# Layer norms from a statistics instruction per 128-column block and one finishing pass shared by two engines

## The chip, the cores and the metric

The kernel runs on one core of one Trainium2 chip. The metric is the time of one execution on the device in microseconds (us), the median of several executions. A profile is one further execution with the hardware profiler on.

## What is computed

The reference runs four graph layers on 6250 nodes of 128 features and 206250 edges, with a layer norm after each of them:

```python
def _layernorm(x, axis=-1, eps=1e-05):
    m = jnp.mean(x, axis=axis, keepdims=True)
    v = jnp.var(x, axis=axis, keepdims=True)
    return (x - m) / jnp.sqrt(v + eps)
...
x = _layernorm(x + _L0_gnn_ref(x, ..., edge_type_3, node_type_3), axis=-1)
x = _layernorm(x + _L1_gnn_ref(x, L1_gnn_weight, L1_gnn_bias, edge_index, edge_weight), axis=-1)
x = _layernorm(x + _L2_gnn_ref(edge_index, x), axis=-1)
x = _layernorm(x + _L3_gnn_ref(x, edge_attr_64, src, dst, 6250, ...), axis=-1)
```

The first layer is a message-passing layer by edge type and node type, the second a hyperbolic one (it begins with the logarithm map of the normed rows, so it needs their norm), the third a normalised sum over neighbours, the fourth a sum over neighbours and edge features with a matrix product and a ReLU.

## The kernel before

The 6250 nodes lie in SBUF as 49 blocks of 128 rows (NB = 49, D = 128): node b*128+p is in partition p, columns b*128 to b*128+127 of the tile `X`, which is 128 partitions by 6272 fp32 columns. `X3` and the other names that end in 3 are the same data seen as 128 x 49 x 128. `big` is one large scratch tile out of which each stage cuts what it needs; in the trace all those cuts are called big. `small` holds vectors of 128 x 49, one number for each node, and `sm(i)` is its i-th slot.

The program is a row of blocks (`nc.Block()`), each with one instruction stream for each engine, and all engines meet at a block's end. Most of the time goes to stages that build and multiply adjacency matrices on TensorE and gather rows on GpSimd. The norms stand between these stages. Norm 1 follows layer 0 and opens the block at L1641; norm 2 is in the block at L1863, behind the hyperbolic layer's last steps; norm 3 is in the block at L2085, a block of VectorE and ScalarE alone; norm 4 is in the last block (L2144), behind the final matrix products, and the store of the output follows it.

`layer_norm` (L665) is a chain on VectorE. It takes the sum of each block (L671; norm 4 has it already, from the accumulator of L2173), divides it (L672), subtracts the mean from all 6272 columns in place (L673), and calls `sum_of_squares` (L658): ScalarE squares the first SHARE = 18 blocks and sums each with its accumulator (L724), while VectorE multiplies the other 31 blocks by themselves (L661) and sums them (L662). Then come the variance (L675), the square root on ScalarE (L721), the reciprocal (L677), in norm 1 the function `logs` (L1650), and the scaling of all 6272 columns into X (L679). `link` makes VectorE wait for each instruction before it starts the next; `Chain` holds the jobs that VectorE asks of ScalarE (`ask`, `did`) and `answer` is ScalarE's side of it. `sum_of_squares` is also called twice outside the norms (L1712, L1871).

Of the kernel before, what the change touches and what calls it, by code (L numbers as in the profile page):

```python
# [20 lines left out]
ALU = mybir.AluOpType  # L21
ACT = mybir.ActivationFunctionType
AX = mybir.AxisListType

P = 128
N, E, D, T, FE = 6250, 206250, 128, 3, 64
NB = -(-N // P)
# [35 lines left out]
EPS = 1e-5  # L63
# [51 lines left out]
def at_least(eng, sem, value):  # L115

    if not isinstance(value, int) or value > 0:
        eng.wait_ge(sem, value)
# [8 lines left out]

BB = 4
SHARE = 18


def in_batches(eng, body):
# [13 lines left out]
def build(nc, x, src, dst, attr, etype, weight, ntype, w_e, b_e, w_n, b_n, w1, b1, w3, w3e, b3, out):  # L146
    ctx = ExitStack()
    with ctx:
        ctx.enter_context(nc.allow_non_contiguous_dma(reason="node types, leftover edges"))

        def sb(name, cols, dt=F32, rows=P):
            return ctx.enter_context(nc.sbuf_tensor(name, [rows, cols], dt))
# [24 lines left out]
        X3 = X[:, :].rearrange("p (b f) -> p b f", b=NB)  # L177
# [26 lines left out]
        small = sb("small", 20 * NB)  # L204
        degs = sb("degs", 6 * NB)
        indeg, outdeg, first_edge, next_edge, row_f, node_id = (degs[:, i * NB:(i + 1) * NB] for i in range(6))
        spill_row = sb("spill_row", NB, I32)
        owner = sb("owner", JB, I32)
        ramp = sb("ramp", P * TU, BF16)
# [439 lines left out]
        def sm(i):  # L649
            return small[:, i * NB:(i + 1) * NB]  # L650

        def along(v):
            return v.unsqueeze(2).to_broadcast([P, NB, D])

        def wide(v):
            return v.rearrange("p (b f) -> p b f", b=NB)

        def sum_of_squares(dve, link, h3, sq3, to):  # L658

            asked = chain.squares(h3, sq3, to)  # L660
            link(dve.tensor_tensor(sq3[:, SHARE:, :], h3[:, SHARE:, :], h3[:, SHARE:, :], ALU.mult))  # L661
            link(dve.tensor_reduce(out=to[:, SHARE:], in_=sq3[:, SHARE:, :], axis=AX.X, op=ALU.add))  # L662
            dve.wait_ge(chain.did, asked)

        def layer_norm(dve, link, h3, sq3, ask_sqrt, before_x=lambda: None, summed=False):  # L665

            mean, var = sm(0), sm(1)
            if not summed:  # L670
                link(dve.tensor_reduce(out=mean, in_=h3, axis=AX.X, op=ALU.add))  # L671
            link(dve.tensor_scalar(mean, mean, 1.0 / D, None, ALU.mult))  # L672
            link(dve.tensor_tensor(h3, h3, along(mean), ALU.subtract))  # L673
            sum_of_squares(dve, link, h3, sq3, var)
            link(dve.tensor_scalar(sm(2), var, 1.0 / D, EPS, ALU.mult, ALU.add))  # L675
            ask_sqrt(sm(2), sm(2))
            link(dve.reciprocal(sm(2), sm(2)))  # L677
            before_x()
            link(dve.tensor_tensor(X3, h3, along(sm(2)), ALU.mult))  # L679

        class Chain:

# [12 lines left out]
            def link(self, ins):  # L695
                self.n += 1
                ins.then_inc(self.v, 1)
                self.dve.wait_ge(self.v, self.n)
# [10 lines left out]
            def squares(self, h3, sq3, to):  # L709
# [3 lines left out]
                self.dve.sem_inc(self.ask, 1)  # L713
                return self.k

            def answer(self, act, first=0, last=None):

                for k, f, i, o, to in self.jobs[first:last]:
                    act.wait_ge(self.ask, k)
                    if f is not None:  # L720
                        act.activation(o, i, f).then_inc(self.did, 1)  # L721
                    else:
                        for b in range(SHARE):
                            made = act.activation(o[:, b, :], i[:, b, :], ACT.Square, accum_out=to[:, b:b + 1])  # L724
                        made.then_inc(self.did, 1)
# [13 lines left out]
        chain = Chain()  # L739
# [901 lines left out]
        with nc.Block() as block:  # L1641
            @block.vector
            def _(dve):
# [6 lines left out]
                def logs():  # L1650
# [8 lines left out]
                    chain.func(ACT.Ln, lo, lo)  # L1659
                    chain.func(ACT.Ln, hi, hi)  # L1660
                layer_norm(dve, link, h43, sq43, chain.sqrt, logs)
                dve.sem_inc(s_x1, 1)
                before_products.append(len(chain.jobs))
# [199 lines left out]
        with nc.Block() as block:  # L1863
            @block.vector
            def _(dve):
                chain.on(dve)
                link = chain.link
                raw, norm, th, f, ne = (sm(i) for i in range(3, 8))
                g = wide(agg7)

                sum_of_squares(dve, link, g, sq83, raw)  # L1871
                chain.sqrt(raw, raw)
                link(dve.tensor_scalar(norm, raw, MIN_NORM, None, ALU.max))
                chain.func(ACT.Tanh, norm, th)
# [260 lines left out]
        h123, sq123 = wide(h12), wide(sq12)  # L2135
# [8 lines left out]
        with nc.Block() as block:  # L2144
            @block.tensor
            def _(pe):
                pe.wait_ge(s_e_rows, 16)
                for b in range(NB):
                    to = ps[b % 8][:, 0:D]
                    at_least(pe, s_a12, b - 7)  # L2150
                    pe.matmul(to, flat[:, b * P:(b + 1) * P], w3s[:, :], start=True, stop=False)  # L2151
                    pe.matmul(to, e_rows[0:FE, b * P:(b + 1) * P], w3ew[:, :], start=False, stop=True).then_inc(s_o12, 1)  # L2152

            @block.vector
            def _(dve):
                chain.on(dve)
                link = chain.link
                for n in range(NB + 2):
                    if n < NB:
                        here = slice(n * D, (n + 1) * D)  # L2160
                        dve.wait_ge(s_o12, n + 1)
                        dve.tensor_tensor(h12[:, here], ps[n % 8][:, 0:D], gained[:, here], ALU.add).then_inc(s_a12, 1)  # L2162
                    if 1 <= n <= NB:
                        b = n - 1
                        here = slice(b * D, (b + 1) * D)
                        dve.wait_ge(s_a12, b + 1)
                        dve.scalar_tensor_tensor(h12[:, here], h12[:, here], degn[:, b:b + 1], b3b[:, :],  # L2167
                                                 ALU.mult, ALU.add).then_inc(s_h12, 1)
                    if n >= 2:
                        b = n - 2  # L2170
                        here = slice(b * D, (b + 1) * D)
                        dve.wait_ge(s_h12, b + 1)
                        dve.scalar_tensor_tensor(h12[:, here], h12[:, here], 0.0, X[:, here], ALU.max, ALU.add,  # L2173
                                                 accum_out=sm(0)[:, b:b + 1]).then_inc(s_r12, 1)
                dve.wait_ge(s_r12, NB)
                layer_norm(dve, link, h123, sq123, chain.sqrt, summed=True)
                dve.sem_inc(s_x4, 1)

            @block.scalar
            def _(act):  # L2180
                chain.answer(act)

            @block.sync
            def _(sp):
                sp.dma_start(e_rows[0:FE, :], e_sums).then_inc(s_e_rows, 16)
                sp.wait_ge(s_x4, 1)
                sp.dma_start(out[0:NFULL * P, :].rearrange("(b p) f -> p b f", p=P), X3[:, 0:NFULL, :]).then_inc(s_out, 16)
                sp.dma_start(out[NFULL * P:N, :], X3[0:NREST, NFULL, :]).then_inc(s_out, 16)
                sp.wait_ge(s_out, 32)
# [20 lines left out]
```

## Time and profile before

| | before |
|---|---|
| timed executions | 5433.2, 5448.58, 5449.89 us; median 5448.58 us |
| profiled execution, its own time | 5436.3 us |
| profiled execution, span | 5434.5 us |
| busy in the span | PE 4035.9 us (74%), DVE 3337.4 us (61%), POOL 2259.1 us (42%), ACT 1187.5 us (22%) |
| granted TensorE clock, mean | 0.932 |

PE is TensorE, DVE VectorE, ACT ScalarE, POOL GpSimd, SP the engine that issues most DMAs. A busy share is a mean over stages with different limits, so what a change in one stage is worth is read from the stretch in which it stands.

### The profile page before, as it was taken

The page shows a single profiled execution, that of the slowest core. Times are in us where ns is not written, and L with a number is a line of the kernel's source. Part 1 is how long each engine was busy: PE and PEld are TensorE (multiplying, and loading weights), DVE is VectorE, ACT ScalarE, POOL GpSimd, SP SyncE. Part 2 cuts the span into 40 slices and gives each one's busy share as a digit, 9 for nine tenths or more (in the row PEclk, how much of TensorE's full clock was granted, in tenths as well). Part 3 has the DMA queues.
Part 4 walks back from the last instruction along what each step waited for, and adds up shares of the span by engine and source line. Part 5 has one row for each costly group of instructions (what it writes and reads, how often), then busy time and mean ns, then how long its engine had stood idle before and what let it go on. Part 6 is the DMA issues. An engine that isn't in the chain of part 4 may idle for free. (4 is left out here: it accounts for less than half of the span.)

```text
span 5434.5 us, 110895 instructions
## 1 busy us (share of the span) xinstructions
PE 4035.9 (74%) x42529; PEld 2913.6 (54%) x42529; DVE 3337.4 (61%) x4224; ACT 1187.5 (22%) x2165; POOL 2259.1 (42%) x2066
## 2 busy tenths in 40 slices
PE   4367755555555554399999995499996799959996
PEld 3255555555555554388888874255554344424444
DVE  7796899898989988566666445666666300150004
ACT  0025555555555554300000000200001100010000
POOL 0051477777777777377777774000000021000200
PEclk9998899999999998799999998699998899979995
DMA  9547687777777778766666665388884566546661
GB/s 306 205 127 252 234 308 274 281 274 291 278 284 276 276 289 243 213 173 174 173 174 173 175 174 107 127 310 305 305 305 146 182 218 211 160 135 206 225 193 49
DMA packets 568380, 1196.81 MB, mean 220 GB/s; under 512 B 173529, under 2 KB 379949, under 8 KB 559117
## 3 DMA queue, kind: packets, MB, share of 16 engines
q1 hardware_dynamic: 481500, 1025.12, 54.4%
q0 software_dynamic: 71088, 153.71, 10.9%
q10 hardware_dynamic: 15660, 16.22, 1.0%
q8 instruction: 85, 1.39, 0.1%
q14 instruction: 47, 0.38, 0.0%
HBM read 767.29 MB, written 480.27 MB: 230 GB/s over the span
## 5 line engine op out<-in xcount | busy, mean ns | idle before, releaser
L1382 PE MATMUL psum<-big 128*128 128x98 bf16 x7936 | 871.9, 209 | 731.5 <-DVE big L1364 534.5
L1336 POOL DMA_INDIRECT big<-typed_msgs,big x1080 | 1258.7, 1165 | 372.6 <-issue 326.7
L1382 PEld LDWEIGHTS psum<-big 128*128 128x128 bf16 x7936 | 772.1, 98 | 782.5 <-issue 303.7
L1979 PE MATMUL psum<-big 128*128 128x512 bf16 (+1 forms) x4704 | 990.5, 374 | 140.4 <-DMA big<-adj 140.4
L1518 POOL DMA_INDIRECT big<-typed_msgs,big x760 | 775.6, 1021 | 322.2 <-issue 224.3
L1383 PE MATMUL psum<-big 128*128 128x49 bf16 x7936 | 858.9, 192 | 0.0
L1384 PE MATMUL psum<-big 128*128 128x49 bf16 x7936 | 855.9, 187 | 0.0
L1979 PEld LDWEIGHTS psum<-big 128*128 128x128 bf16 x4704 | 461.0, 98 | 665.1 <-DMA big<-adj 140.9
L1384 PEld LDWEIGHTS psum<-big 128*128 128x128 bf16 x7936 | 802.9, 102 | 0.0
L1383 PEld LDWEIGHTS psum<-big 128*128 128x128 bf16 x7936 | 776.6, 98 | 0.0
L2026 POOL DMA_INDIRECT big<-spill,spill_row x98 | 92.5, 943 | 1472.0 <-DMA spill<-big 1442.7
L1816 PE MATMUL psum<-big 128*128 128x416 f32 x1984 | 655.7, 494 | 63.5 <-DVE big L1850 62.5
L1364 DVE TENSOR_TENSOR big<-big 128x2400 bf16<-128x2400 bf16 x496 | 694.3, 1400 | 0.0
L1534 DVE SCALAR_TENSOR_TENSOR big<-iota,node,big 128x512 f32<-128x512 f32 x456 | 343.4, 753 | 424.8 <-PE psum L1615 366.5
L1361 DVE TENSOR_TENSOR big<-big 128x2048 bf16<-128x2048 bf16 x496 | 603.5, 1217 | 0.0
L1850 DVE STREAM_TRANSPOSE big<-big 128x3136 f32<-128x3136 f32 x124 | 427.2, 3445 | 239.3 <-PE psum L1816 220.5
L1411 ACT CAST big<-psum 128x784 bf16<-128x784 f32 x496 | 404.8, 816 | 767.4 <-PE psum L1384 486.0
L1615 PE MATMUL psum<-big 128*128 128x128 f32 x3648 | 531.9, 289 | 39.4 <-DMA big<-typed_msgs,big 39.4
L1816 PEld LDWEIGHTS psum<-big 128*128 128x128 f32 x1984 | 377.9, 191 | 340.9 <-issue 82.2
L1615 PEld LDWEIGHTS psum<-big 128*128 128x128 f32 x3648 | 444.6, 192 | 120.2 <-issue 71.4
L1611 PE MATMUL psum<-big 128*64 128x128 f32 x3648 | 498.8, 280 | 6.7 <-DVE big L1534 6.7
L1611 PEld LDWEIGHTS psum<-big 128*64 128x64 f32 x3648 | 388.6, 137 | 86.7 <-issue 43.0
(315 smaller groups left out, 3548.1 us busy)
## 6 DMA issues: line engine op xcount, KB each, us to landing
wadj<-big SPq DMA_DIRECT2D x248, 784.0 KB
big<-wadj SPq DMA_DIRECT2D x124, 1568.0 KB, 7.0
big<-adj SPq DMA_DIRECT2D x210, 896.0 KB, 4.7
adj<-big SPq DMA_DIRECT2D x62, 1568.0 KB
big<-staged SPq DMA_DIRECT2D x266, 256.0 KB
big<-edge_feats SPq DMA_DIRECT2D x456, 128.0 KB
edge_feats<-in_edge_attr SPq DMA_DIRECT2D x1, 51562.5 KB, 162.6
staged<-big SPq DMA_DIRECT2D x30, 1280.0 KB
```

The costliest lines, as they stand in the source:

```text
L1336: pool.indirect_dma_start(out=sgot4[:, c, u, :], out_offset=None, in_=typed_rows, in_offset=bass.IndirectOffsetOnAxis(ap=spair4i[:, c, u, ...
L1361: dve.tensor_tensor(lo_b[:, q, :, :].rearrange("p t (c d) -> p t c d", d=2), in_twos(lo_ramp).to_broadcast([P, TT, P // 2, 2]), all_column ...
L1364: dve.tensor_tensor(hi_b[:, q, :, 1:4, :].rearrange("p t s (c d) -> p t s c d", d=2), hi.unsqueeze(2).to_broadcast([P, TT, 3, HC // 2, 2]) ...
L1382: pe.matmul(to[:, 0:2 * NB], lo, hi_b[:, q, t, 0:2, 0:NB], start=True, stop=False)
L1383: pe.matmul(to[:, NB:2 * NB], lo, hi_b[:, q, t, 2, 0:NB], start=False, stop=False)
L1384: last = pe.matmul(to[:, NB:2 * NB], lo, hi_b[:, q, t, 3, 0:NB], start=False, stop=True)
L1518: pool.indirect_dma_start(out=got4[:, h, u, :], out_offset=None, in_=typed_rows, in_offset=bass.IndirectOffsetOnAxis(ap=pair4i[:, h, u, 0: ...
L1611: pe.matmul(ps[h][0:FE, D:ACCW], feat4[:, h, u, :], hot4[:, k, u, :], start=(u == 0), stop=(u == U - 1))
L1615: last = pe.matmul(ps[h][:, 0:D], hot4[:, k, u, :], got4[:, h, u, :], start=(u == 0), stop=(u == U - 1))
L1816: last = pe.matmul(ps[c][:, 0:(b1 - b0) * 32], rows, turned[:, n % RT, q * QROW + b0 * 32:q * QROW + b1 * 32], start=(m == 0), stop=(m == ...
L1850: dve.transpose(turned[:, n % RT, :].rearrange("p (h i) -> p h i", i=32), wring[:, n % RW, :].rearrange("p (h g) -> p h g", g=32)).then_in ...
L1979: last = pe.matmul(ps[c % 2][:, 0:len(blocks) * P], terms_[:, k, b * D:(b + 1) * D], ring_a[:, m % RA, 0:len(blocks), s * P:(s + 1) * P], ...
```

## The change

`layer_norm` no longer centres the rows nor squares them. VectorE runs its statistics instruction (`bn_stats`) once on each of the 49 blocks. Each gives six numbers for each row: count, mean and sum of squared deviations of the even columns, and the same of the odd columns. Five instructions on 128 x 49 vectors join the two halves into a mean and a sum of squared deviations, two more make the mean's final value and the variance. The square root and the reciprocal stay. One further instruction makes `shift`, minus the mean times the scale. The finishing pass is now one instruction for each block: ScalarE takes the first NORM_SHARE = 19 blocks as Identity with a scale and a bias for each partition (the new job `rows`), VectorE takes the other 30 as subtract and multiply with two scalars for each partition, and then waits for ScalarE. The tile `stats` is new. Norm 4 makes its sums again with the statistics, and L2173 still makes the sum that it no longer uses. `sum_of_squares` and its two other uses stay as they were.

```diff
+NORM_SHARE = 19
...
-            mean, var = sm(0), sm(1)
-            if not summed:
-                link(dve.tensor_reduce(out=mean, in_=h3, axis=AX.X, op=ALU.add))
-            link(dve.tensor_scalar(mean, mean, 1.0 / D, None, ALU.mult))
-            link(dve.tensor_tensor(h3, h3, along(mean), ALU.subtract))
-            sum_of_squares(dve, link, h3, sq3, var)
-            link(dve.tensor_scalar(sm(2), var, 1.0 / D, EPS, ALU.mult, ALU.add))
-            ask_sqrt(sm(2), sm(2))
-            link(dve.reciprocal(sm(2), sm(2)))
+            mean, raw, scale = sm(0), sm(1), sm(2)
+            for b in range(NB):
+                made = dve.bn_stats(stats3[:, b, :], h3[:, b, :])
+            link(made)
+            mean_e, sq_e, mean_o, sq_o = (stats3[:, :, j] for j in (1, 2, 4, 5))
+            link(dve.tensor_tensor(mean, mean_e, mean_o, ALU.add))
+            link(dve.tensor_tensor(scale, mean_e, mean_o, ALU.subtract))
+            link(dve.tensor_tensor(scale, scale, scale, ALU.mult))
+            link(dve.tensor_tensor(raw, sq_e, sq_o, ALU.add))
+            link(dve.scalar_tensor_tensor(raw, scale, D / 4.0, raw, ALU.mult, ALU.add))
+            link(dve.tensor_scalar(mean, mean, 0.5, None, ALU.mult))
+            link(dve.tensor_scalar(scale, raw, 1.0 / D, EPS, ALU.mult, ALU.add))
+            ask_sqrt(scale, scale)
+            link(dve.reciprocal(scale, scale))
+            link(dve.scalar_tensor_tensor(shift, mean, -1.0, scale, ALU.mult, ALU.mult))
             before_x()
-            link(dve.tensor_tensor(X3, h3, along(sm(2)), ALU.mult))
+            asked = chain.rows(h3, X3, scale, shift)
+            for b in range(NORM_SHARE, NB):
+                made = dve.tensor_scalar(X3[:, b, :], h3[:, b, :], mean[:, b:b + 1], scale[:, b:b + 1], ALU.subtract, ALU.mult)
+            link(made)
+            dve.wait_ge(chain.did, asked)
...
+                    if isinstance(f, tuple):
+                        for b in range(NORM_SHARE):
+                            made = act.activation(o[:, b, :], i[:, b, :], ACT.Identity, bias=f[1][:, b:b + 1], scale=f[0][:, b:b + 1])
+                        made.then_inc(self.did, 1)
```

The first place is VectorE's stream at norm 3. Before the change it holds the norm in eight instructions, four of them over 6272 or 3968 columns:

```order
L2094 TENSOR_TENSOR big<-big,X 128x6272
L671 TENSOR_REDUCE small<-big 128x49
L672 TENSOR_SCALAR small<-small 128x49
L673 TENSOR_TENSOR big<-big,small 128x6272
L661 TENSOR_TENSOR big<-big 128x3968
L662 TENSOR_REDUCE small<-big 128x31
L675 TENSOR_SCALAR small<-small 128x49
L677 RECIPROCAL small<-small 128x49
L679 TENSOR_TENSOR X<-big,small 128x6272
```

With the change the same place holds these (lines of the changed kernel):

```order
L2119 TENSOR_TENSOR big<-big,X 128x6272
L675 BN_STATS stats<-big 128x6 x49
L678 TENSOR_TENSOR small<-stats 128x49
L679 TENSOR_TENSOR small<-stats 128x49
L680 TENSOR_TENSOR small<-small 128x49
L681 TENSOR_TENSOR small<-stats 128x49
L682 SCALAR_TENSOR_TENSOR small<-small 128x49
L683 TENSOR_SCALAR small<-small 128x49
L684 TENSOR_SCALAR small<-small 128x49
L686 RECIPROCAL small<-small 128x49
L687 SCALAR_TENSOR_TENSOR stats<-small 128x49
L691 TENSOR_SCALAR X<-big,small 128x128 x30
```

The large instructions are replaced by 49 and 30 of 128 columns each, and six more on vectors stand between them.

The second place is ScalarE's stream at norm 1, where `logs` asks for a logarithm between the square roots and the finishing pass. Before:

```order
L1719 UNCONDITIONAL_BRANCH
L724 ACTIVATE big,small<-big 128x128 x18
L721 ACTIVATE small<-small 128x49 x2
L721 ACT_TABLE_LOAD
L721 ACTIVATE small<-small 128x49 x2
L1727 COPY big<-X 128x128 x4
```

And with the change:

```order
L1744 UNCONDITIONAL_BRANCH
L746 ACTIVATE small<-small 128x49 x2
L746 ACT_TABLE_LOAD
L746 ACTIVATE small<-small 128x49 x2
L743 ACTIVATE X<-big,stats,small 128x128 x19
L1752 COPY big<-X 128x128 x4
```

The 18 squares ahead of the square root are gone, 19 activations into X stand behind the logarithms, and the number of table loads is the same.

## Rows read from the trace of the kernel before

**Rows 1.** The page's first line.

```profile
span 5434.5 us, 110895 instructions
```

**Rows 2.** Windows of the four norms, first instruction to last: length, each engine's busy time.

```profile
3369.12:3402.01 32.89, 0.00 (x0) 0.00 (x0) 30.66 (x14) 7.62 (x41) 0.00 (x0) 0.50 0.00 0
4202.88:4233.05 30.17, 0.00 (x0) 0.00 (x0) 29.48 (x8) 5.62 (x37) 0.00 (x0) 0.50 0.00 0
4777.64:4807.81 30.17, 0.00 (x0) 0.00 (x0) 29.48 (x8) 5.62 (x37) 0.00 (x0) 0.50 0.00 0
5396.86:5420.31 23.45, 0.00 (x0) 0.00 (x0) 22.80 (x7) 5.61 (x37) 0.00 (x0) 0.50 0.00 0
```

**Rows 3.** Timeline of norm 3 on VectorE: start, duration, instruction, idle before.

```profile
4777.64 6.69 DVE L671 TENSOR_REDUCE small<-big 128x49 f32<-128x6272 f32 x1
4784.36 0.19 DVE L672 TENSOR_SCALAR small<-small 128x49 f32<-128x49 f32 x1
4784.59 6.69 DVE L673 TENSOR_TENSOR big<-big,small 128x6272 f32<-128x6272 f32 x1
4791.43 4.29 DVE L661 TENSOR_TENSOR big<-big 128x3968 f32<-128x3968 f32 x1
4795.75 4.29 DVE L662 TENSOR_REDUCE small<-big 128x31 f32<-128x3968 f32 x1
4800.07 0.19 DVE L675 TENSOR_SCALAR small<-small 128x49 f32<-128x49 f32 x1
4800.63 0.46 DVE L677 RECIPROCAL small<-small 128x49 f32<-128x49 f32 x1 [0.37 <-ACT small L721]
4801.12 6.69 DVE L679 TENSOR_TENSOR X<-big,small 128x6272 f32<-128x6272 f32 x1
```

**Rows 4.** Timeline behind norm 3: the next stage's first load and first product.

```profile
4808.70 23.87 SPq L1938 DMA_DIRECT2D big<-adj  x7
...
4815.82 19.37 PE L1979 MATMUL psum<-big 128*128 128x512 bf16 x77 [72.67 <-DMA big<-adj]
```

**Rows 5.** Timeline of norm 1 on VectorE: where `logs` begins, and what follows it.

```profile
3392.61 0.21 DVE L1652 TENSOR_TENSOR small<-small 128x49 f32<-128x49 f32 x1
...
3395.32 6.69 DVE L679 TENSOR_TENSOR X<-big,small 128x6272 f32<-128x6272 f32 x1 [1.03 <-ACT small L721]
```

**Rows 6.** Timeline of VectorE ahead of norm 4: instructions of 128 columns, unlinked.

```profile
5393.93 0.29 DVE L2162 TENSOR_TENSOR big<-psum,big 128x128 f32<-128x128 f32 x1 [0.69 <-PE psum L2152]
5394.14 0.34 DVE L2167 SCALAR_TENSOR_TENSOR big<-big,small,b3b 128x128 f32<-128x128 f32 x1
5394.40 0.28 DVE L2173 SCALAR_TENSOR_TENSOR big<-big,X 128x128 f32<-128x128 f32 x1
5394.61 0.08 DVE L2173 DVE_READ_ACCUMULATOR big<-big,X 128x1 f32 x1
```

**Rows 7.** Timeline of VectorE near the start: linked instructions of 128 columns.

```profile
243.11 0.29 DVE L773 TENSOR_TENSOR big<-b1b 128x128 f32<-128x128 f32 x1 [0.37 <-PEq L376]
243.44 0.29 DVE L774 TENSOR_REDUCE small<-big 128x1 f32<-128x128 f32 x1
...
246.51 0.29 DVE L780 TENSOR_SCALAR b1b<-b1b,small 128x128 f32<-128x128 f32 x1
```

**Rows 8.** Timeline of VectorE after norm 1: linked instructions on vectors.

```profile
3444.94 0.21 DVE L1696 TENSOR_TENSOR small<-small 128x49 f32<-128x49 f32 x1
3445.19 0.19 DVE L1698 TENSOR_SCALAR small<-small 128x49 f32<-128x49 f32 x1
3445.41 0.25 DVE L1699 TENSOR_SCALAR small<-small 128x49 f32<-128x49 f32 x1
```

**Rows 9.** ScalarE: timeline of L1123 and L724; the instructions of L1129 (min/median/max ns).

```profile
367.17 0.27 ACT L1123 COPY big<-psum 128x128 f32<-128x128 f32 x1
...
4791.68 0.29 ACT L724 ACTIVATE big<-big 128x128 f32<-128x128 f32 x1
4791.88 0.19 ACT L724 ACTIVATION_READ_ACCUMULATOR big<-big 128x1 f32 x1
...
L1129 ACT ACTIVATE big<-psum,big x147: 358/398/457, 365.0 to 588.4; 128x128 f32<-128x128 f32 x147
```

**Rows 10.** Groups of VectorE instructions by line: busy us, mean ns, idle before.

```profile
L571 DVE SCALAR_TENSOR_TENSOR big<-big 128x1612 bf16<-128x1612 bf16 x1 | 3.1, 3051 | 0.0
L595 DVE TENSOR_TENSOR big<-big 128x1612 f32<-128x1612 int32 x1 | 1.8, 1826 | 0.0
```

More of the change, by code:

```diff
@@ L206, in build @@
         indeg, outdeg, first_edge, next_edge, row_f, node_id = (degs[:, i * NB:(i + 1) * NB] for i in range(6))
+        stats = sb("stats", 7 * NB)
+        stats3 = stats[:, 0:6 * NB].rearrange("p (b s) -> p b s", s=6)
+        shift = stats[:, 6 * NB:7 * NB]
         spill_row = sb("spill_row", NB, I32)
@@ L663, in sum_of_squares, with layer_norm @@
             dve.wait_ge(chain.did, asked)
-        def layer_norm(dve, link, h3, sq3, ask_sqrt, before_x=lambda: None, summed=False):
-            mean, var = sm(0), sm(1)
-            if not summed:
-                link(dve.tensor_reduce(out=mean, in_=h3, axis=AX.X, op=ALU.add))
-            link(dve.tensor_scalar(mean, mean, 1.0 / D, None, ALU.mult))
-            link(dve.tensor_tensor(h3, h3, along(mean), ALU.subtract))
-            sum_of_squares(dve, link, h3, sq3, var)
-            link(dve.tensor_scalar(sm(2), var, 1.0 / D, EPS, ALU.mult, ALU.add))
-            ask_sqrt(sm(2), sm(2))
-            link(dve.reciprocal(sm(2), sm(2)))
-            before_x()
-            link(dve.tensor_tensor(X3, h3, along(sm(2)), ALU.mult))
+        def layer_norm(dve, link, h3, sq3, ask_sqrt, before_x=lambda: None):
+            mean, raw, scale = sm(0), sm(1), sm(2)
[13 more added lines that the diff above has]
+            link(dve.scalar_tensor_tensor(shift, mean, -1.0, scale, ALU.mult, ALU.mult))
+            before_x()
+            asked = chain.rows(h3, X3, scale, shift)
[3 more added lines that the diff above has]
+            dve.wait_ge(chain.did, asked)
         class Chain:
@@ L714, in squares, with rows @@
                 return self.k
+            def rows(self, h3, x3, scale, shift_):
+                self.k += 1
+                self.jobs.append((self.k, (scale, shift_), h3, x3, None))
+                self.dve.sem_inc(self.ask, 1)
+                return self.k
             def answer(self, act, first=0, last=None):
@@ L719, in answer @@
                     act.wait_ge(self.ask, k)
-                    if f is not None:
+                    if isinstance(f, tuple):
+                        for b in range(NORM_SHARE):
+                            made = act.activation(o[:, b, :], i[:, b, :], ACT.Identity, bias=f[1][:, b:b + 1], scale=f[0][:, b:b + 1])
+                        made.then_inc(self.did, 1)
+                    elif f is not None:
                         act.activation(o, i, f).then_inc(self.did, 1)
@@ L2175, in _ @@
                 dve.wait_ge(s_r12, NB)
-                layer_norm(dve, link, h123, sq123, chain.sqrt, summed=True)
+                layer_norm(dve, link, h123, sq123, chain.sqrt)
                 dve.sem_inc(s_x4, 1)
```

## The prediction

> **What bounds the kernel now.** I read the page first, for the span and the busy shares [rows 1]. VectorE's share there says nothing of the norms, so I took windows over the four norms, from the first instruction of each to the end of its last [rows 2]. They last 32.89, 30.17, 30.17 and 23.45 us, 116.7 us together or 2.1% of the span. In all four TensorE and GpSimd have no instruction and no DMA moves. VectorE is busy for 29.48 of 30.17 us in norms 2 and 3. So the norms are serial: nothing lies beside them but ScalarE's 5.6 us, and that is hidden under VectorE. The timeline of norm 3 shows what fills them [rows 3]: three passes over 6272 columns at 6.69 us and two over 3968 columns at 4.29 us, each waiting for the one ahead. What comes next waits too: the adjacency load is issued 0.9 us after the last pass ends at 4807.81, and TensorE, idle for 72.67 us, starts when it lands [rows 4]. A microsecond saved in a norm is thus a microsecond of the end time, and one lost is lost.
>
> In norm 1 the logarithm steps stand between the reciprocal and the last pass, from 3392.61 to 3395.32, which is 2.71 us [rows 5]. The change leaves them alone. Without them norm 1 is 30.18 us, and the four norms hold 30.18 + 30.17 + 30.17 + 23.45 = 113.97 us that the change touches.
>
> **The new norm, part by part.** Everything is in VectorE's stream, so I price by start-to-start distances, not by durations.
>
> *Statistics.* 49 instructions over 128 columns. The trace has none of this kind. Two nearby forms bound it from below: two-tensor instructions of 128 columns without a link last 0.28 to 0.29 us but start the next one 0.21 us later, since the end of one overlaps the start of the next; even the one with an accumulator to read out keeps that distance [rows 6]. The nearest in kind, a sum over 128 columns, lasts 0.29 us [rows 7]. This one writes six results in place of one, so I take a little more: 0.31 us long and 0.24 us apart. The upper bound has no overlap and a slower rate, and is a rival below. 48 distances of 0.24, one full duration of 0.31 and 0.03 for the link make 11.86 us. They replace L671 to L662.
>
> The Trainium skill, in "VectorE: DVE Perf Modes", section "The TRN2 errata", speaks against this part: it says that instructions on SBUF pay a fixed cost each and that tiles should have 512 columns or more so that the cost is spread. Its formula would put a 128-column instruction at 58 + 128 cycles of 0.96 GHz, an estimate of 0.194 us, and the 49 at 9.5 us in place of my 11.86. So by the page's own figure the fixed cost is real (49 of them in place of one) but smaller than what I count from rows; the rows' 0.21 us is the measured bound.
>
> *Vectors.* Four two-tensor instructions of 49 columns at 0.25 us and one fused one that I put with them, then two with constants at 0.22 us [rows 8]: with the unrounded distance of about 0.245 it is 5 x 0.245 + 2 x 0.22 = 1.67 us. From the second of those two to the reciprocal, ScalarE's square root adds what it adds now: 4800.63 - 4800.07 less the 0.22 already counted is 0.34 us [rows 3]. The reciprocal takes 0.49 us to the next start, and the new instruction for the shift 0.25 us. That makes 1.08 us. ScalarE is ready sooner, as it has no squares to do.
>
> *Finishing pass.* VectorE has 30 instructions of 128 columns. With one scalar for each partition such an instruction lasts 0.29 us [rows 7]; a second one adds what the first adds on 49 columns, 0.25 - 0.19 = 0.06 us [rows 8], so 0.35 us, and with the overlap of some 0.08 us that rows 6 show (0.34 long, 0.26 apart) 0.27 us apart. 29 x 0.27 + 0.35 + 0.03 is 8.21 us. ScalarE has 19. A square on SBUF lasts 0.29 us and frees the engine after 0.20; a bias for each partition makes a PSUM read of 128 columns 0.358 us in place of 0.27, about 0.09 more [rows 9]. With two such operands the 19 stand 0.385 us apart and the last lasts 0.48: 18 x 0.385 + 0.48 + 0.09 for the start is 7.50 us, hidden under VectorE's 8.21. If that cover went (VectorE at its lower bound of 0.21 apart), ScalarE's 7.50 would be the end of the pass: 0.7 us better for each norm and no more. No table load is added: ScalarE's stream has as many as before, and the one in norm 1 stands where it stood.
>
> *Sum.* 11.86 + 1.67 + 1.08 + 8.21 = 22.82 us for each norm, 91.3 us for four against 113.97. The saving is 22.7 us: 7.35 us in each of the first three and 0.6 us in norm 4, where the sum was free before. Most of it is L673's pass of 6.69 us, which has no successor. The statistics with their joining steps (13.5 us) take 1.7 us less than the sum and the two passes of the squares (15.3 us) [rows 3], and the finishing pass takes 1.5 us more than now. Outside the norms nothing moves: the other two sums of squares are untouched, the scratch of the new tile is 7 x 49 columns, and no engine's stream gains a wait on another but for the 19 activations, behind which nothing is queued before VectorE's own end.
>
> Against the profiled execution's own time of 5436.3 us this gives 5413.6. The timed executions shown lie at 5433.2, 5448.58 and 5449.89 us, so the median stands 12.3 us above the profiled one, and from it the same saving gives 5425.9. The scatter of the executions is as large as half the effect. I take the middle, 5420 us, 6 us from either. About 0.3% (16.3 us) is what a measurement of this kernel can tell from no change.
>
> **Rivals.**
> *The statistics instructions do not overlap, or run slower than a column a cycle.* If each waits for the one ahead, the distance is that of linked instructions, 243.44 - 243.11 = 0.33 us [rows 7]. It costs 192 x 0.09 = 17.3 us, and the saving shrinks to 5.4 us: 5431 from the profiled time, 5443 from the median. A slower rate has a precedent too: L571 takes 3051 ns for as many columns as L595 does in 1826 [rows 10], 0.76 ns more a column, 97 ns for 128; 192 x 0.097 is 18.6 us, saving 4.1 us. For it: a running mean and squared deviation need more steps on a column than a sum. Against it: every unlinked pair in the rows overlaps. Chance 0.27. The Trainium skill, in "Vector Engine (DVE) Microarchitecture Reference", section "State that persists across instructions", names the batch-norm statistics as a reader of a parameter memory that "self-orders" with earlier and later instructions of VectorE. I read that as a reason for such an instruction to wait for its neighbours; no run here shows it yet, and the time would be the 5431 to 5443 just given.
>
> *Six results cost like six read-outs: slower than before.* One accumulator read lasts 0.08 us [rows 6]. If the end of each statistics instruction took five more of them in series, the distance would be 0.64 us: 192 x 0.40 = 77 us lost, 54 us slower than before, 5490 us. It decides from a distance of 0.358 us on (22.7 / 192 = 0.118 above mine), and shows as slower by over 0.3% from 0.443. Against it: rows 6 hide the one read-out wholly under the next instruction. Chance 0.10.
>
> *The finishing pass is the costly one.* If 30 instructions with two scalars don't overlap, they stand 0.38 us apart: 4 x 29 x 0.11 = 12.8 us lost, saving 9.9 us, 5426 to 5439. For it: no unlinked pair with two scalars is in the trace. Against: one scalar did not hinder the overlap in rows 6. Chance 0.05.
>
> **How the numbers follow.** The forecast, distances of 0.21 to 0.30 us, holds 0.58. With the lower bounds (0.21 for the statistics, 5.8 us, and the pass at ScalarE's end, 2.8 us) the saving is 31 us, 5405 from the profiled time. The rival without overlap ends at 5443 on the median. So the range is 5405 to 5443. It leaves out the read-out case, part of the forecast's and the first rival's tails, together 2 in 10. Faster by over 0.3% needs a distance up to 0.273: most of the forecast's 0.58 and little else, 0.55. Within 0.3%: the first and third rival and the forecast's upper end, 0.34. Slower: the read-out case and some scatter, 0.11.
>
> **What would show it.** The first start to start distance in the row of statistics: 0.24 us right, 0.33 the first rival, over 0.44 the second. The pass: 30 instructions in about 8.2 us and ScalarE's 19 ending some 0.7 us before them. Windows over the norms: 22.8 us each, norm 1 with its logarithms 25.5. The wait of the next stage's product should be shorter by the 7.35 us and by nothing else. I would be wrong if a statistics instruction lasted 0.4 us or more, or if the stages around the norms changed length.

## The result and the profile after

The changed kernel takes 5403.89 us (median of 6 executions, 5398.89 to 5410.81) against 5437.91 us for the kernel before (median of 6 in all, 5433.2 to 5449.89). The medians are 34.0 us apart; the ratio is 0.9934, with a 95% interval of 0.9921 to 0.9948, so the gain lies between 28 and 43 us. Executions over 1.5% above a kernel's fastest are left out of the comparisons; these are two of the kernel before in the last series of experiments, 7195.73 and 7212.64 us. I had forecast 5420 us and a saving of 22.7 us; the measured time lies 1 us below the range's lower end. The direction was right and the saving half as large again as forecast.

The windows over the four norms of the changed kernel, first instruction to last, answer to [rows 2] (columns: length, busy time and count of PE, PEld, DVE, ACT, POOL, granted clock, DMA share, GB/s):

```profile
3369.42:3392.47 23.05, 0.00 (x0) 0.00 (x0) 20.72 (x94) 9.68 (x24) 0.00 (x0) 0.50 0.00 1
4192.08:4212.43 20.35, 0.00 (x0) 0.00 (x0) 19.55 (x88) 7.66 (x20) 0.00 (x0) 0.50 0.00 0
4757.08:4777.41 20.33, 0.00 (x0) 0.00 (x0) 19.54 (x88) 7.66 (x20) 0.00 (x0) 0.50 0.00 0
5366.53:5386.88 20.35, 0.00 (x0) 0.00 (x0) 19.56 (x88) 7.66 (x20) 0.00 (x0) 0.50 0.00 0
```

They were 32.89, 30.17, 30.17 and 23.45 us. The differences are 9.84, 9.82, 9.84 and 3.10 us, 32.6 us together. The page's first line gives the span:

```profile
span 5401.2 us, 111146 instructions
```

It was 5434.5 [rows 1], so 33.3 us went, and 32.6 of them went inside the norms. The mean granted TensorE clock of this execution was 0.904, where the profile of before has 0.932. That is not the gain: of the 31 executions of the kernel before that go with experiments 1 to 4, those near 0.90 and those near 0.93 have the same median to 0.1 us (5438.4 us), and of the six of the changed kernel the one at 0.934 took 5404.16 us. The timeline of norm 3 on VectorE, which answers to [rows 3] (start, length of the row, instruction, how many):

```profile
4757.08 9.57 DVE L675 BATCH_NORM_STATS2 stats<-big 128x6 f32<-128x128 f32 x49
4766.68 0.24 DVE L678 TENSOR_TENSOR small<-stats 128x49 f32<-128x49 f32 x1
4766.96 0.24 DVE L679 TENSOR_TENSOR small<-stats 128x49 f32<-128x49 f32 x1
4767.24 0.21 DVE L680 TENSOR_TENSOR small<-small 128x49 f32<-128x49 f32 x1
...
4768.23 0.19 DVE L684 TENSOR_SCALAR small<-small 128x49 f32<-128x49 f32 x1
4768.78 0.46 DVE L686 RECIPROCAL small<-small 128x49 f32<-128x49 f32 x1 [0.37 <-ACT small L746]
4769.28 0.21 DVE L687 SCALAR_TENSOR_TENSOR stats<-small 128x49 f32<-128x49 f32 x1
4769.64 7.77 DVE L691 TENSOR_SCALAR X<-big,small 128x128 f32<-128x128 f32 x30 [0.15 <-DVE stats L687]
```

And ScalarE beside it, with the durations of the two finishing instructions from their own views (min/median/max ns):

```profile
4769.58 7.41 ACT L743 ACTIVATE X<-big,stats,small 128x128 f32<-128x128 f32 x19 [0.83 <-DVEq L734]
...
L675 DVE BATCH_NORM_STATS2 stats<-big x196: 271/276/294, 3369.4 to 5375.8; 128x6 f32<-128x128 f32 x196
...
L691 DVE TENSOR_SCALAR X<-big,small x120: 331/339/348, 3384.7 to 5386.5; 128x128 f32<-128x128 f32 x120
```

A row that groups n equal instructions gives their start-to-start distance: its length less one duration, divided by n - 1. The statistics stand (9.57 - 0.276) / 48 = 0.194 us apart, though each lasts 0.276; the finishing instructions (7.77 - 0.339) / 29 = 0.256 us. ScalarE ends at 4776.99, VectorE at 4777.41, so the share of 19 blocks hides with 0.4 us to spare. The next stage follows as before: its load is issued at 4778.29 and TensorE starts at 4785.19, 7.8 us behind the norm's end, where it was 8.0 us [rows 4]. TensorE's wait ahead of it is 62.60 us in place of 72.67: 10.1 us shorter, with the norm 9.84 us shorter.

```profile
4778.29 3.20 SPq L1963 DMA_DIRECT2D big<-adj  x4
...
4785.19 12.05 PE L2004 MATMUL psum<-big 128*128 128x512 bf16 x43 [62.60 <-DMA big<-adj]
```

### The profile page after: what moved, and what is told of

Its sections match the earlier page's. It is cut to its first block and busy times, and to the rows that moved or that the text cites. A ratio compares the mean times of both kernels' runs of the same rounds, so it can differ in the third digit from the quotient of the medians.

```text
span 5401.2 us, 111146 instructions
## 1 busy us (share of the span) xinstructions
PE 4039.3 (75%) x42529; PEld 2915.4 (54%) x42529; DVE 3304.5 (61%) x4545; ACT 1194.5 (22%) x2097; POOL 2248.4 (42%) x2066
## 5 line engine op out<-in xcount | busy, mean ns | idle before, releaser
L1361 POOL DMA_INDIRECT big<-typed_msgs,big x1080 | 1253.0, 1160 | 372.5 <-issue 327.9
L2051 POOL DMA_INDIRECT big<-spill,spill_row x98 | 92.4, 943 | 1453.4 <-DMA spill<-big 1424.1
L1438 ACT COPY big<-psum 128x784 f32<-128x784 f32 x496 | 434.1, 875 | 0.0
```

The source lines that it names most:

```text
L1361: pool.indirect_dma_start(out=sgot4[:, c, u, :], out_offset=None, in_=typed_rows, in_offset=bass.IndirectOffsetOnAxis(ap=spair4i[:, c, u, ...
L1438: act.copy(wadj_st[:, k, b // 2, :, b % 2 * TT:(b % 2 + 1) * TT], made_in(b % 2)[:, :, NB:2 * NB].rearrange("p t s -> p s t")).then_inc(s_ ...
```

## The experiments

Two theories stood against each other. Theory A: the norms are serial, so the time is the sum of start-to-start distances in them and reaches the end one for one. Theory B: part of the gain comes from stages around them, or is scatter.

**1. The statistics alone.** The new statistics, then two passes over all columns, nothing on ScalarE but the square root.

```diff
-            link(dve.scalar_tensor_tensor(shift, mean, -1.0, scale, ALU.mult, ALU.mult))
...
-            asked = chain.rows(h3, X3, scale, shift)
-            for b in range(NORM_SHARE, NB):
...
+            link(dve.tensor_tensor(h3, h3, along(mean), ALU.subtract))
+            link(dve.tensor_tensor(X3, h3, along(scale), ALU.mult))
```

> The statistics instruction is kept, the finishing pass goes back to two passes over 6272 columns (subtract the mean, then multiply by the scale), no ScalarE share. Theory A (the norms are serial, so the saving is the sum of start-to-start distances and reaches the end one for one): a norm is 9.6 + 2.6 + 2 x 6.7 = 25.6 us; against 30.17 it saves 4.6 us in each of norms 1 to 3 and loses 2.2 in norm 4, 11.5 us in all, ratio 0.998. Theory B (part of the change's gain comes from the stages around the norms, which start earlier or run otherwise): the time outside the norms moves by several us too, and the windows over the norms do not add up to the difference of the spans.

Measured: 5425.69 us against 5438.43 (10 and 31 executions), ratio 0.9977 with an interval of 0.9952 to 1.0002. The interval includes 1, so the time alone does not show a gain; its size comes from the windows. In norm 3 the statistics begin at 4776.99 and the last pass ends at 4795.92 + 6.69 = 4802.61: 25.62 us.

```profile
4776.99 9.57 DVE L675 BATCH_NORM_STATS2 stats<-big 128x6 f32<-128x128 f32 x49
...
4789.20 6.69 DVE L688 TENSOR_TENSOR big<-big,small 128x6272 f32<-128x6272 f32 x1
4795.92 6.69 DVE L689 TENSOR_TENSOR X<-big,small 128x6272 f32<-128x6272 f32 x1
```

**2. The finishing pass alone.** The old sums, but of uncentred rows, with the mean's square taken off afterwards; the centring pass is gone, and the new finishing pass stands at the end. Norm 4 has its sum for nothing again, as before the change.

```diff
+            if not summed:
+                link(dve.tensor_reduce(out=mean, in_=h3, axis=AX.X, op=ALU.add))
+            link(dve.tensor_scalar(mean, mean, 1.0 / D, None, ALU.mult))
+            sum_of_squares(dve, link, h3, sq3, raw)
+            link(dve.tensor_tensor(scale, mean, mean, ALU.mult))
+            link(dve.scalar_tensor_tensor(raw, scale, -float(D), raw, ALU.mult, ALU.add))
```

> The old sums stay (one pass for the sum, 31 blocks squared and summed on VectorE, 18 on ScalarE), but of the rows as they are, with the mean's square taken off afterwards, so that the centring pass is gone; then the new finishing pass. Theory A: 6.7 + 0.2 + 8.6 + 1.8 + 7.9 = 25.3 us for norms 1 to 3 and 18.6 for norm 4, so 4.9 us saved in each of the four, 19.5 us, ratio 0.9964. Were the statistics what pays (a rival), this one would save next to nothing.

Measured: 5416.9 us against the same 5438.43, ratio 0.9959 (0.9942 to 0.9975). Norm 3 runs from 4763.84 to 4781.45 + 7.77 = 4789.22: 25.38 us.

```profile
4763.84 6.69 DVE L675 TENSOR_REDUCE small<-big 128x49 f32<-128x6272 f32 x1
...
4770.90 4.29 DVE L665 TENSOR_TENSOR big<-big 128x3968 f32<-128x3968 f32 x1
4775.23 4.29 DVE L666 TENSOR_REDUCE small<-big 128x31 f32<-128x3968 f32 x1
...
4781.45 7.77 DVE L687 TENSOR_SCALAR X<-big,small 128x128 f32<-128x128 f32 x30 [0.15 <-DVE stats L683]
```

In norms 1 to 3 the two halves of the change are worth about the same: 4.79 us here, where the centring pass goes, and 4.55 us in experiment 1, where the statistics replace the sum and the squares. In norm 4 this half still saves 4.79 us and the statistics lose 2.2, as the sum was free there; so over four norms it is 19.2 us against 11.5. Together the halves save more than their sum in norms 1 to 3 (9.8 against 9.3), since two steps of 0.24 us were added here for the variance (4779.55 to 4780.04).

**3. No share for ScalarE.** All 49 blocks of the finishing pass on VectorE.

```diff
-            for b in range(NORM_SHARE, NB):
+            for b in range(NB):
```

> The changed kernel with all 49 blocks of the finishing pass on VectorE. Theory A: 19 more instructions at 0.256 us in each norm, 4 x 19 x 0.256 = 19.5 us slower than the changed kernel, saving 13 to 14 us against before, ratio 0.9975. Rival (ScalarE and VectorE get into each other's way on SBUF, so that the share buys little): the 0.256 us between two VectorE instructions falls clearly, towards 0.20, once ScalarE is still.

Measured: 5423.75 us, ratio 0.9968 (0.9953 to 0.9983). The 49 take 12.64 us, the distance is (12.64 - 0.338) / 48 = 0.256 us, what it was beside a busy ScalarE. So ScalarE does not slow VectorE's pass, and the rival falls. (No run has ScalarE's 19 beside an idle VectorE, so the other direction is not shown.)

```profile
4779.54 12.64 DVE L690 TENSOR_SCALAR X<-big,small 128x128 f32<-128x128 f32 x49
```

**4. A wait behind each statistics instruction**, the first rival of the prediction made real.

```diff
-                made = dve.bn_stats(stats3[:, b, :], h3[:, b, :])
-            link(made)
+                link(dve.bn_stats(stats3[:, b, :], h3[:, b, :]))
```

> The changed kernel with a wait behind every statistics instruction. The case of my first rival made real: a statistics instruction that waits for the one ahead. Theory A: distance 0.276 + 0.04 = 0.316 us in place of 0.195, 4 x 48 x 0.121 = 23 us slower than the changed kernel, saving 10 us against before, ratio 0.998. If the instructions ordered themselves already (the rival), the wait would add only some 0.02 us each, 4 us.

Measured: 5430.24 us, ratio 0.9978 (0.9962 to 0.9994). The 49 take 16.05 us, a distance of (16.05 - 0.294) / 48 = 0.328 us against 0.194 without the wait. My rival's price of 0.33 us was right for instructions that wait; the changed kernel's don't wait.

```profile
4761.95 16.05 DVE L675 BATCH_NORM_STATS2 stats<-big 128x6 f32<-128x128 f32 x49
```

These four and the changed kernel test theory A in numbers. Norm 3's window stands for norms 1 to 3; in the experiments norm 4 is the same, but for experiment 2, where it lacks the sum (6.72 us from the row of L675 to the next). Saving by windows against saving by medians, in us:

| kernel | norm 3 | norm 4 | saving by windows | by medians |
|---|---|---|---|---|
| before | 30.17 | 23.45 | | |
| changed | 20.33 | 20.35 | 32.6 | 34.0 |
| 1 statistics alone | 25.62 | 25.62 | 11.5 | 12.7 |
| 2 finishing pass alone | 25.38 | 18.66 | 19.2 | 21.5 |
| 3 no share | 25.08 | 25.08 | 13.6 | 14.7 |
| 4 linked statistics | 26.82 | 26.82 | 6.7 | 8.2 |

The order and the sizes agree, each within 2.4 us. The medians say more than the windows in all five, by 1.0 to 2.4 us; this is not explained, and it is all that theory B could claim. The intervals of the ratios are 15 to 27 us wide, so that the medians come so close is in part luck; the windows are the finer measure.

Single spans would mislead here:

```profile
span 5431.0 us, 110948 instructions
...
span 5419.1 us, 111146 instructions
```

These are experiments 1 and 4. The spans are 3.5 and 15.4 us shorter than before, the norms 11.5 and 6.7 us. What is left lies outside the norms, much of it ahead of any changed instruction: norm 1 starts at 3378.45 us in experiment 1, 3366.04 in experiment 4, 3369.12 before and 3369.42 in the changed kernel. The stretch between norms 1 and 2 varies too, 794.7 us in experiment 4 and 800.9 before, while the stretches behind it agree to 1.6 us in all six kernels. So that before and after differ by 33.3 us in span and by 32.6 us in the norms is a closer match than one execution of each gives by itself.

**5. Distances measured by themselves.** Test instructions into scratch, ahead of norm 3 of the changed kernel (one execution, 7220.09 us, taken for its profile).

```diff
+                for b in range(NB):
+                    t = dve.tensor_tensor(sq93[:, b, :], h93[:, b, :], X3[:, b, :], ALU.add)
+                link(t)
...
+                for n in (64, 256, 512):
+                    for b in range(12):
+                        t = dve.bn_stats(stats3[:, b, :], h9[:, b * n:(b + 1) * n])
+                    link(t)
```

> The changed kernel with test instructions into scratch ahead of norm 3: 49 of 128 columns each of an add of two SBUF tiles, the same with a semaphore increment on each, the same with one tile from PSUM, a sum over the columns, a multiply with accumulator, a multiply-add with constants, a multiply-add with one scalar for each partition; then 12 statistics instructions each of 64, 256 and 512 columns. Theory P (on SBUF each instruction without a wait costs 58 cycles and a cycle a column, 0.194 us at 128; my row of 0.21 us was larger since it read PSUM or had something beside it): the plain add stands 0.194 us apart, the PSUM one 0.21, statistics of 64, 256 and 512 columns 0.127, 0.327 and 0.594. Theory Q (the statistics instruction is cheaper than a two-tensor one as it writes six columns only): the plain add stands 0.21 apart like the rows of before, and 64 columns of statistics cost less or more than 0.127.

The timeline (an add; the same with semaphore increments; with one tile in PSUM; a sum; the first and the last of a multiply with accumulator; a multiply-add with constants; with one scalar for each partition), and behind it the statistics by shape, first as timeline, then as groups (busy us, mean ns):

```profile
6446.75 9.99 DVE L2122 TENSOR_TENSOR big<-big,X 128x128 f32<-128x128 f32 x49
6456.77 9.99 DVE L2126 TENSOR_TENSOR big<-big,X 128x128 f32<-128x128 f32 x49
6466.79 9.79 DVE L2129 TENSOR_TENSOR big<-psum,X 128x128 f32<-128x128 f32 x49
6476.61 9.56 DVE L2132 TENSOR_REDUCE small<-big 128x1 f32<-128x128 f32 x49
6486.21 0.29 DVE L2135 SCALAR_TENSOR_TENSOR big<-big,X 128x128 f32<-128x128 f32 x1
...
6496.41 0.29 DVE L2135 SCALAR_TENSOR_TENSOR big<-big,X 128x128 f32<-128x128 f32 x1
...
6496.74 6.72 DVE L2139 TENSOR_SCALAR big<-big 128x128 f32<-128x128 f32 x49
6503.50 9.69 DVE L2142 TENSOR_SCALAR big<-big,small 128x128 f32<-128x128 f32 x49
...
6513.22 1.62 DVE L2146 BATCH_NORM_STATS2 stats<-big 128x6 f32<-128x64 f32 x12
...
6514.88 4.02 DVE L2146 BATCH_NORM_STATS2 stats<-big 128x6 f32<-128x256 f32 x12
...
6518.93 7.22 DVE L2146 BATCH_NORM_STATS2 stats<-big 128x6 f32<-128x512 f32 x12
...
L2146 DVE BATCH_NORM_STATS2 stats<-big 128x6 f32<-128x512 f32 x12 | 7.2, 677 | 0.0
L2146 DVE BATCH_NORM_STATS2 stats<-big 128x6 f32<-128x256 f32 x12 | 4.0, 411 | 0.0
L2146 DVE BATCH_NORM_STATS2 stats<-big 128x6 f32<-128x64 f32 x12 | 1.6, 215 | 0.0
```

| 128 columns, unlinked | distance, us |
|---|---|
| multiply-add with constants | 0.136 |
| the same, one scalar for each partition | 0.196 |
| the same, two (the finishing pass) | 0.256 |
| sum over the columns | 0.193 |
| statistics | 0.194 |
| two tensors, SBUF, with or without increments | 0.202 |
| two tensors, one in PSUM | 0.198 |
| two tensors and accumulator (6486.21 to 6496.41 for 48) | 0.213 |

The statistics of 64, 256 and 512 columns stand (1.62 - 0.215) / 11 = 0.128, 0.328 and 0.595 us apart, which is theory P to within 1 ns. That theory was the formula of the Trainium skill, "VectorE: DVE Perf Modes", section "The TRN2 errata" (58 cycles and a cycle a column at 0.96 GHz). For two tensors it is 8 ns too low here, and one tile in PSUM costs nothing more (0.198 us), where P had 0.21. Theory Q is half right: the statistics are cheaper than two tensors, by 8 ns, but the plain add stands 0.202 apart and not 0.21, and 64 columns are where P had them. That they write few columns is not shown as the reason: the multiply-add with constants writes 128 and stands 0.136 apart. The 0.21 us that I took as a lower bound was no bound for this kind.

**6. Statistics twice, the last statistics early, and the sums shared.** In the series of experiments 5 to 8 the kernel before took 7142.86 us, and in the last one, on the same chip as experiments 1 to 4, 7143.81 (median of 33). Of the surplus of 1.7 ms, 1.6 lie ahead of norm 1: in the changed kernel's profile there its first full-width pass starts at 4965.0 us where it started at 3362.7, and the gathers of L1361 on GpSimd take 1849 ns in place of 1160. VectorE's rows in the norms are the same to 10 ns. Why those executions are longer was not settled. The standard error of a mean of 8 to 12 executions is 5 to 10 us there, so two kernels that are less than some 20 us apart (an estimate, twice the error of a difference of 10) are not told apart by time.

```profile
L1361 POOL DMA_INDIRECT big<-typed_msgs,big x1080 | 1996.5, 1849 | 788.8 <-DMA big<-edge_pairs 466.1 <-issue 322.6
...
7060.52 9.57 DVE L675 BATCH_NORM_STATS2 stats<-big 128x6 f32<-128x128 f32 x49
...
7073.09 7.78 DVE L691 TENSOR_SCALAR X<-big,small 128x128 f32<-128x128 f32 x30 [0.15 <-DVE stats L687]
```

(These rows are of the changed kernel in the last series.)

Statistics twice, so that a norm does 49 of them for nothing:

```diff
+            for turn in range(2):
-            for b in range(NB):
-                made = dve.bn_stats(stats3[:, b, :], h3[:, b, :])
+                for b in range(NB):
+                    made = dve.bn_stats(stats3[:, b, :], h3[:, b, :])
```

> The changed kernel with the 49 statistics instructions made twice in each norm. Theory A (serial, one for one): 4 x 9.6 = 38.4 us more than the changed kernel, about 5 us slower than before, ratio 1.001. Rival (some of the norms' time hides under other work): less than 30 us more.

> Statistics twice in each norm. Theory A: 38.4 us more than the changed kernel in this series, 5 us more than before, ratio 1.001; the rival of hidden time less than 30 us more.

Measured: 7145.09 us, ratio 0.9991 (0.9963 to 1.0019), and again 7141.77, ratio 1.0012 (0.9977 to 1.0048). In the last series it is 35.6 us over the changed kernel's 7106.16 by medians. The 98 in norm 4 of that series take 19.18 us, 9.6 more, and the four norms together 122.6 us against 84.1: 38.4 us, the size that theory A gave. The medians agree with it, but their scatter alone could not rule out the rival's 30 us.

```profile
7084.12 19.18 DVE L676 BATCH_NORM_STATS2 stats<-big 128x6 f32<-128x128 f32 x98
```

The last norm's statistics inside the loop over the final products; the accumulator that nothing uses goes with it:

```diff
-                for n in range(NB + 2):
+                for n in range(NB + 3):
...
+                    if n >= 3:
+                        dve.wait_ge(s_r12, n - 2)
+                        made = dve.bn_stats(stats3[:, n - 3, :], h123[:, n - 3, :])
...
-                                                 accum_out=sm(0)[:, b:b + 1]).then_inc(s_r12, 1)
```

> The changed kernel, where the statistics of the last norm are made inside the loop over the 49 final products, a block behind its last addition, in the 0.69 us that VectorE waits for TensorE in each turn, and the accumulator that nothing uses is gone. Theory A: 9.5 us leave the end, saving 42 us against before, ratio 0.9923. Rival (the 0.2 us more in each turn holds up the reading of PSUM, so that TensorE waits): the loop grows by up to 49 x 0.2 = 9.8 us and nothing is won.

> Statistics of the last norm inside the loop over the final products. Theory A: from the profiles so far the turn of the loop stays at 1.45 us and VectorE's wait in it shrinks from 0.69 to 0.49 us, so 9.5 us less than the changed kernel, 42 us less than before, ratio 0.992.

Measured: 7089.46 us, ratio 0.9942 (0.9913 to 0.9972), and again 7107.85, ratio 0.9937 (0.9902 to 0.9972). Both are faster than before, but by time alone it can't be told from the changed kernel, whose median in the same series was 7106.16. The profile tells it. A turn of the loop on VectorE (first profile of this kernel):

```profile
7062.47 0.29 DVE L2188 TENSOR_TENSOR big<-psum,big 128x128 f32<-128x128 f32 x1 [0.49 <-PE psum L2178]
7062.67 0.34 DVE L2193 SCALAR_TENSOR_TENSOR big<-big,small,b3b 128x128 f32<-128x128 f32 x1
7062.93 0.28 DVE L2199 SCALAR_TENSOR_TENSOR big<-big,X 128x128 f32<-128x128 f32 x1
7063.14 0.29 DVE L2203 BATCH_NORM_STATS2 stats<-big 128x6 f32<-128x128 f32 x1
7063.91 0.29 DVE L2188 TENSOR_TENSOR big<-psum,big 128x128 f32<-128x128 f32 x1 [0.49 <-PE psum L2178]
```

The turn is 7063.91 - 7062.47 = 1.44 us, as before the change (5391.04 to 5392.48 us there), and the wait for TensorE in it is 0.49 us where [rows 6] has 0.69. From the first of the products to the last finishing instruction it is 83.6 us (6995.8 to 7079.4) against 92.4 us in the changed kernel (5294.1 to 5386.5): 8.8 us are gone, with TensorE no slower (69.8 us from first product to last in both). The last series repeats it, 83.6 us (7031.2 to 7114.8) against 92.5 (6988.0 to 7080.5). Norm 4's window itself is 9.6 us shorter (10.74 us in place of 20.35), so the loop and its end took 0.8 us more, and not the rival's 9.8.

```profile
L2176 PE MATMUL psum<-w3s,big x98: 420/502/581, 5294.1 to 5363.9; 128*128 128x128 f32 x98
...
L2177 PE MATMUL psum<-w3s,big x98: 421/501/582, 6995.8 to 7065.6; 128*128 128x128 f32 x98
...
L692 DVE TENSOR_SCALAR X<-big,small x120: 336/340/347, 4989.0 to 7079.4; 128x128 f32<-128x128 f32 x120
```

(The first of these rows is of the changed kernel, the others of this one.)

ScalarE's part in the statistics, added to that:

```diff
+                asked = chain.sums(h3, sq3, mean, raw)
+                for b in range(k, NB):
...
+                        for b in range(STAT_SHARE):
+                            act.activation(o[:, b, :], i[:, b, :], ACT.Identity, scale=2.0 / D, accum_out=to[0][:, b:b + 1])
+                            made = act.activation(o[:, STAT_SHARE + b, :], i[:, b, :], ACT.Square, accum_out=to[1][:, b:b + 1])
```

> As the one with the early last statistics, and in norms 1 to 3 ScalarE, idle until the square root, makes sum and sum of squares of 12 of the 49 blocks by two activations with accumulators each (12 x 0.59 = 7.0 us), VectorE the statistics of 37 (37 x 0.194 = 7.2 us), with three short steps more to join them (0.6 us). Theory A: 2.4 less 0.6 is 1.8 us saved in each of three norms, 5 us in all, 47 us against before, ratio 0.9914. Rival: the activations with accumulators run slower beside VectorE's statistics, or start late, and the 5 us are not there.

> As the one before, and ScalarE makes the sums of 12 blocks in norms 1 to 3. Theory A: 1.8 us less in each of three norms, 5 us less than the one before, 47 us less than the kernel before, ratio 0.9914; its rival, that nothing is won, gives the time of the one before.

Measured: 7076.37 us, ratio 0.9915 (0.9882 to 0.9948), and again 7091.48, ratio 0.9928 (0.9894 to 0.9961): the lowest median of both series. Norm 3's window, and in it VectorE's part and ScalarE's first instruction:

```profile
6437.48:6455.84 18.36, 0.00 (x0) 0.00 (x0) 17.50 (x78) 14.72 (x68) 0.00 (x0) 0.50 0.00 0
...
6437.43 0.31 ACT L758 ACTIVATE big<-big 128x128 f32<-128x128 f32 x1 [35.04 <-DVEq L749]
6437.48 7.25 DVE L679 BATCH_NORM_STATS2 stats<-big 128x6 f32<-128x128 f32 x37
```

18.36 us in place of 20.33: 1.97 us in each of three norms, where 1.8 were expected. ScalarE's activations keep their 0.29 us beside the statistics, but for the first (0.31). By windows this version saves 32.6 + 8.8 + 3 x 1.97 = 47 us; the times (66 and 52 us by medians, with their scatter) don't speak against it, but don't measure it either, and don't tell it from the version before.

The changed kernel in the last series:

> The changed kernel itself, beside the three that follow. The four of the series before ran on a chip on which the kernel before took 7143 us, 31% more than on the others, so three of them are timed again. Theory A: 33 us less than before, ratio 0.9940. Theory B (part of the first measurement's difference was scatter between executions, since its medians are 34 us apart with 17 us of scatter): 23 to 30 us less.

Measured: 7106.16 us, ratio 0.9949 (0.9916 to 0.9983). The interval holds the 33 us and the 23 us alike, so for the size the first measurement and the windows stand.

## Why the prediction was off

**Right:** the mechanism. The norms are serial and a microsecond in them is one at the end, to the 1.0 to 2.4 us of the table. The parts were right: joining steps and square root came out at 2.96 us (4766.68 to 4769.64) against my 2.75, ScalarE's 19 activations at 7.41 us, as in my sum, hidden with 0.4 us where I had 0.7. The stretches outside the norms sum to 5317.1 us against 5317.8 before, and the next stage's start kept its distance. (The passes over 6272 or 3968 columns that the change replaces are five, as the prediction counts them; the text on the change says four.)

**The step that failed** is the size of one term, that of the statistics: I put them 0.24 us apart, they stand 0.194 apart. That is 9.60 us for a norm against 11.86, 9.0 us over four norms, and nearly the whole gap between 22.7 and 32.6. Two choices were wrong in it. I took two-tensor instructions as the nearest form and their 0.21 us as a lower bound. And I added 0.03 us for six results. The work on a column and the six results cost nothing over a plain sum: 0.194 us against 0.193 in experiment 5. The nearest row in kind was the sum over 128 columns, of which the trace of before had only linked ones [rows 7]; its duration of 0.29 less the overlap of 0.08 that I used for the finishing pass would have given 0.21 too, so the rows alone did not reach 0.194, and the formula of the Trainium skill ("VectorE: DVE Perf Modes", section "The TRN2 errata"), which I weighed and set aside, did. Since the bound was no bound, the range ended too early: its lower end allows a saving of 31 us, and the norms gave 32.6.

**The finishing pass** was mis-sized the same way by little: 0.256 us apart, not 0.27, 0.4 us for each norm. Against these two, the joining steps took 0.2 us more than forecast: the ones that read every sixth column of the statistics last 0.24 us, not 0.21, and 0.15 us of idle stands ahead of the pass. 2.26 + 0.44 - 0.21 is the 2.49 us by which a norm is shorter than my 22.82.

**The base** cost some microseconds too. I stood between the profiled 5436.3 us and a median of 5448.58 from three executions; with six the median was 5437.91, with 31 others 5438.43. The profiled time was the better guide. With it alone my forecast would have been 5413.6 us, still 10 us high, and 5405 as its lower end was the same. So of the 16 us that the forecast was off, 6.4 are the base and the rest is the sum; both erred the same way.

**The rivals:** statistics that wait for each other have the price that I gave (0.328 us in experiment 4, forecast 0.33), but they don't do it. The Trainium skill's "self-orders" ("Vector Engine (DVE) Microarchitecture Reference", section "State that persists across instructions") thus shows in no such wait here: with nothing between them the distance is that of a plain sum. A slower rate than that of a plain pass is excluded: from 64 to 512 columns a column costs (0.595 - 0.128) / 448 = 1.04 ns, and a pass over 6272 columns takes 6.69 us, 1.07 ns a column. Six read-outs in series would have put them 0.64 us apart, and the third rival the pass 0.38 us; they stand 0.194 and 0.256 apart.

## What to carry to other kernels

Price a run of small VectorE instructions by start-to-start distance of the same kind of sources: here statistics and sums of 128 columns stood 0.194 us apart, two tensors 0.202, a multiply-add with constants 0.136, and each scalar for each partition added 0.06; the duration in the row (0.28 us for statistics) is not the price. Before replacing passes by a clever instruction, ask what the passes are for: dropping the centring pass, by folding the mean into the last one, paid as much in each norm as the statistics instruction did (4.8 and 4.6 us), and it paid in norm 4 too, where the statistics lost. And where a loop waits for TensorE, work of the next step can stand in that wait for next to nothing: the last norm's statistics cost 9.6 us behind the loop and 0.8 us in it.

## What the runs showed of the hardware that was not expected

A statistics instruction over 64 to 512 columns costs 0.128 to 0.595 us unlinked, a straight line with 0.061 us plus 1.04 ns a column, though it makes mean and squared deviations of two halves. A wait between such instructions costs 0.134 us each (0.328 against 0.194), which is two thirds of the instruction. A multiply-add of one SBUF tile takes 0.136 us for 128 columns with constants and 0.196 with one scalar for each partition, so the two scalars of the finishing pass (0.256) cost nearly as much as its work. Reading one tile from PSUM was no slower than from SBUF (0.198 against 0.202). And some series of executions ran 31% longer, nearly all of it ahead of the norms, while VectorE's durations in the norms stayed the same; this was not explained.
